# Moving TensorE's broadcast of B from the end to the beginning of each slot of a scan

## The reference, cut to what matters

```
Bm, Cm = xb @ W_b, xb @ W_c                 # 16 states each
delta  = softplus(xb @ W_delta + b_delta)   # 512 channels
h = exp(delta * A) * h + delta * Bm * xb    # per token, channel and state
y = sum over the states of h * Cm, + xb * Dp
out = (y * silu(z)) @ W_out
```

## Time and profile before

| | us |
|---|---|
| median of 3 runs | 4367.42 |
| lowest, highest run | 4363.86, 4371.5 |
| the profiled execution, its own time | 4363.94 |
| its span in the trace | 4361.8 |
| TensorE busy in the span | 3551.9 |
| VectorE busy | 3312.0 |
| ScalarE busy | 2208.1 |
| GpSimd busy | 1346.1 |

### The profile page before, as it was taken

One profiled execution on the slowest core, in us unless ns is written; L12 is line 12 of the kernel. 1 busy time (PEld: TensorE's weight loads), 2 busy tenths in 40 slices (PEclk: granted clock), 3 DMA queues, 4 the chain that ended last, 5 costly groups with the idle time before them and its releaser, 6 DMA issues. The chain is left out here.

```text
span 4361.8 us, 49461 instructions
## 1 busy us (share of the span) xinstructions
PE 3551.9 (81%) x14625; PEld 1613.8 (37%) x14625; DVE 3312.0 (76%) x3753; ACT 2208.1 (51%) x3556; POOL 1346.1 (31%) x372
## 2 busy tenths in 40 slices
PE   3228778688587785876898599999999999999898
PEld 1014435345344343443555032323232232323565
DVE  5988878888888788878731787878787787878444
ACT  4325444445444433544421077777777777777321
POOL 2755565555565555656620000000000000000110
PEclk8569979889798897898999599999999999999999
DMA  2011112212112121121211300000000000000101
GB/s 93 27 32 41 63 40 65 64 33 86 51 56 61 40 74 61 39 81 41 85 57 50 96 16 17 23 17 16 16 23 17 16 16 20 20 17 16 32 29 34
DMA packets 110764, 183.13 MB, mean 42 GB/s; under 512 B 14495, under 2 KB 84599, under 8 KB 101817
## 3 DMA queue, kind: packets, MB, share of 16 engines
q1 hardware_dynamic: 110521, 180.09, 13.3%
HBM read 153.95 MB, written 26.09 MB: 41 GB/s over the span
## 5 line engine op out<-in xcount | busy, mean ns | idle before, releaser
L1585 DVE TENSOR_REDUCE tile_max<-ps 128x1 f32<-128x1024 f32 x1076 | 1268.2, 1220 | 288.3 <-PE ps L1376 285.6
L1530 ACT ACTIVATE probs<-ps 128x512 f32<-128x512 f32 x2056 | 1116.6, 598 | 493.2 <-PE ps L1390 468.1
L1131 POOL TENSOR_TENSOR h<-h,c_sb 128x2048 f32<-128x2048 f32 x128 | 596.6, 4661 | 909.5 <-DVE state L937 909.5
L1390 PE MATMUL ps<-qs,ks 101*128 101x512 bf16 x2056 | 713.2, 385 | 1.2
L1376 PE MATMUL ps<-ks,qs 99*128 99x512 bf16 x2152 | 669.0, 393 | 48.9 <-DMA ks<-scratch_kb 41.1
L930 DVE TENSOR_TENSOR_SCAN h<-decay,state,ps 128x512 f32<-128x512 f32 x512 | 627.5, 1267 | 23.9 <-ACT decay L669 1.4
L498 PE MATMUL ps<-x1T,e_w 128*128 128x512 f32 x1024 | 520.1, 661 | 118.2 <-ACT hid L740 95.6
L1141 POOL TENSOR_TENSOR y_sum<-y_sum,h 128x2048 f32<-128x2048 f32 x128 | 589.2, 4603 | 19.9 <-ACT y_sum L677 9.8
L1400 PE MATMUL ps<-probs,vh 128*32 128x512 f32 x4096 | 552.0, 611 | 24.6 <-issue 24.6
L518 PE MATMUL ps<-e_w,hid 128*128 128x256 f32 x2048 | 454.6, 380 | 12.6 <-ACT hid L740 7.5
L1702 POOL COPY vh<-v_all 128x256 f32 (+1 forms) x32 | 12.7, 402 | 1434.4 <-PE ps L1400 1369.0
(11 more groups left out here) (172 smaller groups left out, 3222.6 us busy)
## 6 DMA issues: line engine op xcount, KB each, us to landing
e_w<-in_e_w SPq DMA_DIRECT2D x64, 1024.0 KB, 7.0
c_sb<-scratch_c SPq DMA_DIRECT2D x128, 256.0 KB, 3.5
qs<-scratch_q SPq DMA_DIRECT2D x210, 64.0 KB
ks<-scratch_k SPq DMA_DIRECT2D x210, 64.0 KB
scratch_q<-parts SPq DMA_DIRECT2D x16, 384.0 KB, 4.1
scratch_k<-parts SPq DMA_DIRECT2D x16, 384.0 KB, 7.4
xr<-scratch_x SPq DMA_DIRECT2D x10, 512.0 KB, 4.0
xn_tok<-in_x SPq DMA_DIRECT2D x8, 512.0 KB, 4.8
```

The costliest lines, as they stand in the source:

```text
L1131: nc.gpsimd.tensor_tensor(h[:, n % 2], h[:, n % 2], c_sb[:, n % C_RING:n % C_RING + 1, :].to_broadcast([P, DB, CH]), ALU.mult).then_inc(s[ ...
L1390: mm(ps[:, S_BANK[i], :], ks[0:K_ALL, j, step * P:(step + 1) * P], qs[0:K_ALL, j, qc * CH:(qc + 1) * CH], start=True, stop=True).then_inc( ...
L1530: fn(probs[:, step % 2, qc, :], ps[:, S_BANK[i], :], ACT.Exp)\
L1585: v.tensor_reduce(tile_max[:, t, half:half + 1], ps[:, slot(side):slot(side) + PAIR, :].rearrange("p a n -> p (a n)"), AX.X, ALU.max).then ...
```

## The change

The loop over the slots gets the broadcast of state n + 2 as its first statement, and the same two lines near its end go. The broadcasts of the next chunk's states 0 and 1, in slots 14 and 15, stay at the end. Nothing else is changed.

```diff
--- before.py
+++ after.py
@@ -592,6 +592,8 @@
                 if isinstance(i, int) and i == 1:
                     pe.wait_ge(s["w_moe"], W_MOE)
                 for n in range(NS):
+                    if inside(i) and n + 2 < NS:
+                        broadcast(i, n + 2)
                     if n == 0 and inside(q):
                         down(q, NE - 1, 1)
                     if n == 1 and inside(m):
@@ -647,8 +649,6 @@
                         project_delta(f, 2 * (n - 13) + 1)
                     if n == 8 and inside(q):
                         key_bias(q, i)
-                    if inside(i) and n + 2 < NS:
-                        broadcast(i, n + 2)
                     if inside(f) and n + 2 >= NS:
                         broadcast(f, n + 2 - NS)
 
```

## The result

The changed kernel takes 4552.28 us (median of 4 runs, 4543.88 to 4553.48), the kernel before 4369.46 us in the same comparison; the ratio is 1.0416, 95% interval 1.0398 to 1.0434. It is slower by 183 us, all of it in the first program, whose last VectorE instruction starts at 2605.0 us in the one trace and at 2416.2 in the other. The profiled execution took 4553.48 us, with a span of 4551.3; it lies 189.5 us above the profiled one of the kernel before (4363.94), a little more than the medians do. The prediction was 4556, a range of 4495 to 4630.

A forecast was written before the change was run, and what follows sets the result against it. No engine is full; a chain between engines, mainly TensorE and VectorE, sets the period. Each of iterations 1 to 7 loses 27 us, 7 x 27 = 189; 4367.4 + 189 = 4556 us, range 4495 to 4630.

The forecast's parts named there:

- The wait, not the place: TensorE, slots 0 to 13: early broadcasts take their wait along, and all the slot's matmuls queue behind it; iteration +27 us.
- Slots 0 to 2: Last down projection waits for VectorE's second multiply of slot 0, starts cold, takes 9.39 us, not 7.07; VectorE +1.6 us.
- M(3): M(n) is the end of VectorE's second multiply of slot n; M(3) was to move from 1170.5 to 1172.1.
- Slot 3: All its TensorE work, q and k included, follows M(3), about 21 us; it ends near 1193.6, +15.3 us.
- Their own relief: VectorE's cross products (L1034): GpSimd's add is through by then, so they take 2.1 us, not 5.1.
- Slots 6 to 12: TensorE falls behind again after cold starts and a 2.1 us wait for M(10); delay grows from +16.1 to +27.0 us.
- Slots 13 to 15: TensorE waits some 12 us for M(13); delta starts at 1414.7, not 1378.95; delta and du end +27 us.
- stretched: Rival, chance 0.10: delay as worked out, but GpSimd's work moves along and keeps stretching VectorE's instructions: 4633 us.
- The 10 us for iteration 1 in the lower bound: Loss allowed for iteration 1, which has no attention work, in the bound of some 130 us, 4497 us.
- the relief at delta: Iteration's end: delta and du no longer overlap GpSimd's last multiply and add, 13.24 us before; 8.4 us of relief.
- absorbed: Rival, chance 0.05: TensorE's idle time and VectorE as busiest engine let later matmuls be in time; 4367 to 4373 us.
- The price of half clock: TensorE restarts cold after waits, 0 to 2.3 us each; three on the path, in slots 3, 8 and 13.

The follow-up runs named there:

- slots 0 to 2: Kernel before with the broadcast moved to the slot's start only in slots 0, 1 and 2: 4366.10 against 4367.97 us, ratio 1.0001.
- the broadcast behind q and k: Kernel before with slot 3's broadcast moved between the q and k projections and the turn of x1: 4399.96 against 4363.19 us, ratio 1.0085.
- the kernel with slots 6 to 12: Kernel before with the broadcast moved to the slot's start only in slots 6 to 12: 4468.51 against 4367.97 us, ratio 1.0238.
- the experiment on slots 4 and 5: Kernel before with the broadcast moved to the slot's start only in slots 4 and 5: 4398.59 us, ratio 1.0086.
- the parts: Kernels before with the broadcast early only in slots 0 to 2 (no change), 3 (+79 us), 4 and 5 (+35), 6 to 12 (+101), 13 (+9.3).
- the early silu: ScalarE's silu of the convolution in slot 10 instead of 11: kernel before 4345.28 against 4364.86 us; changed kernel 4516.67 us.

## Why the prediction was right

The forecast was 4556 and the kernel takes 4552. The mechanism held; that the number came within 4 us is in part luck, because terms that were too large met iterations that lose more than the sample. By its own steps:

- The wait, not the place. Confirmed by slots 0 to 2 (151 us of new waits, no cost) and by the broadcast behind q and k (half the cost of the one ahead of them).
- Slots 0 to 2: +1.6 forecast for M(3). 1248.66 - 1189.90 = 58.76 against 1170.55 - 1112.44 = 58.11: +0.65. The down projection took 8.52 us, not 9.39, and stopped VectorE for 0.90.
- Slot 3: its end +15.3 forecast, 13.1 measured (1268.89 - 1189.96 = 78.9, against 65.85). The work took 20.2 us, not 21.5 with its broadcast, and started 1 us earlier; so the cross products came 13.1 us late, not 15.3. Their own relief was right: with the line behind them they took 5.1 us and were to take 2.1, they take 2.0 (from 1279.89 to 1281.9).
- Slots 6 to 12: the stop in slot 9 was forecast at 3.7 us and is 3.60; the wait for M(10) 2.1 us, measured 2.11; from the logits to slot 12 I had 10.9 us, measured are 11.1 (13.0 to 24.1). That these agree hides errors of both signs: up to M(8) the delay was 0.4 us less than forecast, between M(8) and the end of slot 9 the delay grew 1.4 us more than forecast, since eight matmuls behind a wait of 2.97 us took 5.40 us (the row at 1369.38 above; 3.70 in the same place before), and in slots 10 and 11 0.8 less. Of that 0.8, 0.4 is an error in adding up: 1308.4 + 2.1 + 38.9 is 1349.4, not 1349.8.
- Slots 13 to 15: TensorE was to wait 12 us, it waited 12.21; slots 13 and 14 were to take 32.6 us and took 31.4; delta and du were to take 4.9 us and up to 0.5 us of overlap, they take 5.9. This leaves no room for the rival "stretched", by which they would have stayed at 13 us. Behind du VectorE stands 1.14 us before its next multiply, where it stood 0.27; no term had this.
- One iteration: +27 forecast. The sample gives 310.9 - 285.6 = 25.3. By the starts of delta, iterations 2 to 5 take 311.7 us on average, where it was 284.1: +27.6; iteration 1 +26.2, iteration 6 +24.2, and from the last start of delta to the end of the program 26.4. Iteration 0 takes 194.6 us in both traces, as forecast. I had let iteration 1 lose less and iteration 7 more, so that they cancel. Neither did: both lose about as much as the others (iterations 2, 3 and 5 lose 28 to 29 us). How each comes to its loss was not worked out (iteration 7, in the kernel with slots 6 to 12, loses 21.7 us there alone). The 10 us for iteration 1 in the lower bound were too few by 16.
- The chain of terms was right, the sizes less so. The delay up to the logits was sized 3.1 us too large per iteration (16.1 against 13.0, of it 1.0 in slots 0 to 2, 1.2 in slot 3 and 0.9 in slot 5), slots 13 and 14 by 1.2; the relief at delta was 0.6 to 1.0 smaller than forecast. By its own ends (1414.7 + 4.9 against 1392.2) the forecast was 27.4; less 3.1 and 1.2, plus 0.2 up to slot 12, 0.2 on ScalarE's way to delta, 1.0 in the pair and 0.9 behind du it is the 25.3 of the sample. The sample is the longest iteration of the kernel before (285.6 us, where iterations 2 to 5 have 284.1 on average), and three of the others lose about 3 us more than it: that made up for the terms that were too large. So the two profiled executions lie 189.5 us apart, where 189 were forecast, and the medians 183.
- The rival "absorbed", by which VectorE as the busiest engine sets the time (the Trainium skill, Perfetto Trace Analysis, "Identifying the Most-Contended Engine"), fell: in the sample iteration VectorE was the busiest in both kernels, became less busy (239 to 229 us), and the time rose.

The price of half clock was undersized in one place: I counted it after waits of 4 us and more, and the experiment on slots 4 and 5 shows it after 3.75. The row at 1227.71 in the earlier trace rows, 5.40 us behind a wait of 3.00, had shown it already. In the changed kernel slot 5's wait is 0.32 us, since slot 3 had already made TensorE late, so the omission did not reach the forecast. In part for the same reason the parts do not add up: 0 + 79 + 35 + 101 + 9 = 224 us, and the whole is 183.

## What to carry to other kernels

In an engine that works in order, a moved wait cost here what stood behind it and had been hidden until then, not its own length: list the work behind it and who reads it first. Where two engines hand work to and fro, moving a wait ahead of the work takes away the one slot by which one engine could run ahead, and the exchanges then show (VectorE's stops in slots 9 to 11 here). A wait that grows in the profile after is no proof of a cost: two of the three that grew here (the broadcasts of slots 0 to 2, the scans' wait for decays) could be made or removed for nothing.

## What the runs showed of the hardware that I had not expected

Behind a wait of 3.0 us TensorE can start at half clock or at full, in one and the same kernel. In the first program of the kernel before, eight matmuls of 128x512 of L498 stand behind a wait of 2.88 to 3.00 us for ScalarE 16 times: they took 3.70 us four times and 5.26 to 6.75 us twelve times. In slot 11 of the kernel before with the early silu they took 5.40 to 6.78 us in six iterations and 3.70 in the seventh, in the changed kernel with the same edit 3.70 in four of seven.

The broadcast tells the clock too: 0.38 to 0.39 us where the granted clock is 1.00 (the rows at 1201.55 and 1385.91 of the changed kernel), 0.61 where it is 0.50 (1189.96 and 1344.92). In the changed kernel's iteration shown above it took 0.39 behind waits of 2.11 and 2.56 us, 0.61 behind 5.69 and more. Behind the router's logits (L468, 32 matmuls that put out four columns each, at a granted clock of 1.00) it took 0.61 with a wait of only 1.82 us, in all seven iterations, and 0.59 with none in the kernel before, in six of seven (the row at 1208.46 in the earlier trace rows, granted clock 0.50); in the seventh it took 0.38. Why is open.
